# An attention stage that handles its two heads one after the other, with double-buffered score banks and weights, instead of side by side

## The chip, the cores and the metric

The kernel runs as one program on all 8 cores of one Trainium2 chip. Each core computes its own share and no core waits for another. The metric is the device time of the slowest core in microseconds (us), lower is better. The engines are TensorE (PE in the profile, PEld for its weight loads), ScalarE (ACT), VectorE (DVE), GpSimd (POOL) and SyncE (SP). SyncE only issues DMAs here, and GpSimd too.

## What is computed

The input x has the shape (4, 8192, 1024). Cut to what matters:

```python
xn = layernorm(x)
# attention, 16 heads of 64, 4096 keys and values, the same for every batch
q = relu(xn @ Wq.T + bq); k = relu(keys @ Wk.T + bk); v = relu(values @ Wv.T + bv)
a = softmax(q_h @ k_h.T / 8) @ v_h          # per head
a = transpose(a, (0, 1, 3, 2)).reshape(q.shape)
s = a + xn
# mixture of 8 experts, top 2, then a layernorm, then silu
g = silu(layernorm(xn + sum_e w_e * (relu(xn @ W1_e.T + b1_e) @ W2_e.T + b2_e)))
y = x + s * g
```

Core c takes batch c // 2 and, of it, 8 of the 16 heads with all 8192 queries. Because a head's result is transposed and reshaped, 8 heads are exactly 4096 rows of the output, so that each core finishes its own 4096 rows.

## The kernel before, in words

The program is written engine by engine: each stage has one block of instructions per engine (`@blk.tensor`, `@blk.scalar` and so on), and the order in a block is the order on that engine. Semaphores (`wait_ge`, `bump`) tie them together. There is no scheduler. The stages are, in order: keys and values projected (K transposed in `KT`, V in `VV`, both resident), phase A (layernorm, Q projected and stored to `d_qts`), the attention stage, and the expert stage. The change touches the attention stage alone.

**Work of the attention stage.** There are four head pairs `hp`. A pair has its 64 + 64 rows of Q in one tile `bQ` (128 partitions, 8192 queries). A pair runs 16 query tiles `qt` of 512 queries. A query tile runs 16 groups `gr`, each of two chunks of 128 keys. For one group TensorE multiplies four score products, alternately for head A on partitions 0 to 63 (L547, into `pScA`) and head B on partitions 64 to 127 (L550, into `pScB`). ScalarE turns `pScA` and then `pScB` (128 x 1024 each) into exponentials in `bEx` (L600, L603). TensorE then multiplies them with `bVE`, V with a column of ones, into `pAvA` and `pAvB` (L561; the last group L574), of which row 64 is the softmax's denominator. There is one `pScA` and one `pScB`, and the scores of a group wait for both exponentials of the group before. TensorE issues the values' products of a group after the scores of the next one.

**End of a query tile.** VectorE copies `pAvA` and `pAvB` out in four copies (L645 to L648), rows to `bAssy` and denominators to `bDnS`. The next tile's first score waits for all four. GpSimd bounces them to HBM in three DMAs in a row, each waiting for the one before (L482, L486, L490). `bAssy` has two halves, so the copies of a tile wait for the bounce of two tiles earlier.

**End of a pair (the head tail).** For each of its two heads SyncE loads `bXr` (2 MB of x), the denominators `bD8` (L517) and the bounced result `bScr` (2 MB, L523). TensorE repeats the denominators over the partitions (L586, L587, `pDb`), VectorE takes the reciprocal (L653), multiplies (L658) and adds (L663), ScalarE normalizes x (L611) and then issues the store of `bScr` to `d_ss` (L618). There is one of each buffer, so that the second head's loads wait for the first head's adds and store. After both, VectorE fills `bVE` for the next pair (L632), from which the next pair's first score waits.

**The casts.** GpSimd's block begins each pair with four DMAs, two of W1 and two of W2 (L473, L476), each reading 16 MB of fp32 weights and writing 8 MB of bf16 for the expert stage. They wait only for the one before of the same kind, and stand ahead of the pair's bounces.

Of the kernel before, what the change touches and what calls it, by code (L numbers as in the profile page):

```python
# [17 lines left out]
S = 8192  # L18
# [20 lines left out]
def build_program():  # L39
# [37 lines left out]
    with ExitStack() as st0:  # L77
        def sb(name, shape, dt):
            return st0.enter_context(nc.sbuf_tensor(name, shape, dt))
        def sem(name):  # L80
            return Ctr(st0, nc, name)
# [32 lines left out]
        c_qT = sem("c_qT"); c_xr = sem("c_xr"); c_d8 = sem("c_d8"); c_scr = sem("c_scr")  # L114
# [326 lines left out]
        def sc_cnt(hp, qt, gr):  # L441
            return (hp * NQT + qt) * NGR + gr + 1
        def ex_cnt(hp, qt, gr):
            return ((hp * NQT + qt) * NGR + gr + 1) * 2
        def av_cnt(hp, qt, gr):
            return (hp * NQT + qt) * NGR + gr + 1
        def ae_cnt(hp, qt):
            return (hp * NQT + qt + 1) * 4
        def bn_cnt(hp, qt):
            return 48 * (hp * NQT + qt + 1)  # L450

        with ExitStack() as stb:
            bQ = stb.enter_context(nc.sbuf_tensor("bQ", [128, S], BF16))
            bVE = stb.enter_context(nc.sbuf_tensor("bVE", [128, 2 * 32 * 65], BF16))
            bEx = stb.enter_context(nc.sbuf_tensor("bEx", [128, 4 * 1024], BF16))
            bAssy = stb.enter_context(nc.sbuf_tensor("bAssy", [128, 2 * 512], F32))
            bDnS = stb.enter_context(nc.sbuf_tensor("bDnS", [1, 4 * 512], F32))
# [4 lines left out]
            pScA = stb.enter_context(nc.psum_tensor("pScA", [128, 1024], F32))  # L462
            pScB = stb.enter_context(nc.psum_tensor("pScB", [128, 1024], F32))
            pAvA = stb.enter_context(nc.psum_tensor("pAvA", [128, 512], F32))
            pAvB = stb.enter_context(nc.psum_tensor("pAvB", [128, 512], F32))
# [3 lines left out]
            def _(g):  # L469
                for hp in range(4):  # L470
# [7 lines left out]
                    for qt in range(NQT):  # L478
                        g.wait_ge(b_ae.h, ae_cnt(hp, qt))
                        sl = qt % 2  # L480
                        g.wait_ge(c_bn.h, c_bn.n)
                        g.dma_start(out=d_bnc[:, qt * 512:(qt + 1) * 512],  # L482
                                    in_=bAssy[:, sl * 512:(sl + 1) * 512]).then_inc(c_bn.h, 16)
                        c_bn.n += 16
                        g.wait_ge(c_bn.h, c_bn.n)
                        g.dma_start(out=d_bncr2[0:1, qt * 512:(qt + 1) * 512],  # L486
                                    in_=bDnS[0:1, (sl * 2) * 512:(sl * 2 + 1) * 512]).then_inc(c_bn.h, 16)
                        c_bn.n += 16
                        g.wait_ge(c_bn.h, c_bn.n)
                        g.dma_start(out=d_bncr2[1:2, qt * 512:(qt + 1) * 512],  # L490
                                    in_=bDnS[0:1, (sl * 2 + 1) * 512:(sl * 2 + 2) * 512]).then_inc(c_bn.h, 16)
                        c_bn.n += 16
            W1CAST, W2CAST = c_w1.n, c_w2.n

            @blk.sync
            def _(sync):
                for hp in range(4):
# [5 lines left out]
                    if hp >= 1:  # L503
                        sync.wait_ge(b_sc.h, sc_cnt(hp - 1, NQT - 1, NGR - 1))
                    c_qT.bump(sync.dma_start(out=bQ[:], in_=d_qts[hp]), 16)
                    for a in range(2):
# [7 lines left out]
                        sync.wait_ge(c_bn.h, bn_cnt(hp, NQT - 1))  # L514
# [16 lines left out]
            def _(t):  # L531
                for hp in range(4):
                    t.wait_ge(c_qT.h, 16 * (hp + 1))
                    t.wait_ge(b_ve.h, 2 * (hp + 1))
                    for qt in range(NQT):
                        if qt >= 1:
                            t.wait_ge(b_ae.h, ae_cnt(hp, qt - 1))
                        elif hp >= 1:
                            t.wait_ge(b_ae.h, ae_cnt(hp - 1, NQT - 1))
# [579 lines left out]
```

## Time and profile before

| | us |
|---|---|
| median of 4 runs | 13927.75 (13821.23 to 14802.28) |
| the other two runs | 13857.45, 13998.06 |
| the profiled execution, its time | 13778.97 |
| the profiled execution, its span on the slowest core | 13777.0 |
| spans of the eight cores | 13734.0 to 13777.0 |

The profile is one execution, recorded on core 0. Its time and its span differ by 2 us. All rows shown are of that core. In a row of the timeline the columns are: start in us, duration in us, engine, line and operation, output and inputs, how many instructions are merged, and in brackets how long the engine stood idle before it and what ended that. "PEclk" is the granted TensorE clock as a share of 2.4 GHz, so 0.50 is the lower level of 1.2 GHz.

### The profile page before, as it was taken

The page shows a single profiled execution, that of the slowest core. Times are in us where ns is not written, and L with a number is a line of the kernel's source. Part 1 is how long each engine was busy: PE and PEld are TensorE (multiplying, and loading weights), DVE is VectorE, ACT ScalarE, POOL GpSimd, SP SyncE. Part 2 cuts the span into 40 slices and gives each one's busy share as a digit, 9 for nine tenths or more (in the row PEclk, how much of TensorE's full clock was granted, in tenths as well). Part 3 has the DMA queues.
Part 4 walks back from the last instruction along what each step waited for, and adds up shares of the span by engine and source line. Part 5 has one row for each costly group of instructions (what it writes and reads, how often), then busy time and mean ns, then how long its engine had stood idle before and what let it go on. Part 6 is the DMA issues. An engine that isn't in the chain of part 4 may idle for free.

```text
span 13777.0 us, 118078 instructions; the slowest of 8 cores (13734.0 to 13777.0 us)
## 1 busy us (share of the span) xinstructions
PE 9561.0 (69%) x43120; PEld 4159.8 (30%) x43808; DVE 2433.7 (18%) x5384; ACT 4015.3 (29%) x4988; POOL 159.4 (1%) x297
## 2 busy tenths in 40 slices
PE   3235552254055135499799799799799799798897
PEld 1124110011011011144344344344344344343343
DVE  0345000000000000211211211211211211212212
ACT  1232562365066146411211211211211211211212
POOL 0000000000000000000000000000000000000000
PEclk7675896688589678799899899899899899899998
DMA  8521005401800720144344344344344344343343
GB/s 115 102 72 65 19 5 65 81 6 18 127 6 6 85 61 6 53 147 147 141 150 147 129 149 152 130 150 150 135 147 150 140 148 150 128 150 141 141 150 116
DMA packets 244726, 1438.74 MB, mean 104 GB/s; under 512 B 25581, under 2 KB 66806, under 8 KB 108102
## 3 DMA queue, kind: packets, MB, share of 16 engines
q1 hardware_dynamic: 178646, 1176.04, 23.7%
q0 software_dynamic: 39920, 204.77, 10.6%
q10 hardware_dynamic: 25600, 50.34, 1.0%
q8 instruction: 367, 6.01, 0.2%
q14 instruction: 193, 1.58, 0.0%
HBM read 1517.84 MB, written 201.59 MB: 125 GB/s over the span
## 4 chain that ended last, share of the span: by engine, by line
PE 60%; ACT 17%; another core or an unknown queue 10%; DVE 8%; issue 4%; DMA 1%; ACTq 0%; DVEq 0%; SPq 0%; POOLq 0%
PE pO L819 26%; PE pH L799 25%; ACT bEx L600 8%; ACT bEx L603 7%; PE pScA L547 5%; DVE aXnT L325 1%; PE pQL L425 1%; PE pQL L417 1%; DVE aSm L295 1%; DVE aVar L303 1%; PE pScB L550 0%; DVE aXnT L329 0%; PE pTr L409 0%; DMA bD<-bncr 0%
## 5 line engine op out<-in xcount | busy, mean ns | idle before, releaser
L799 PE MATMUL pH<-cXnT,cW 128*128 128x512 bf16 x16053 | 3560.8, 381 | 241.0 <-ACT cHR L852 222.2
L819 PE MATMUL pO<-cHW,cW 128*128 128x512 bf16 x16053 | 3538.3, 379 | 108.8 <-DVE cHW L942 91.0
L852 ACT ACTIVATE cHR<-pH,cB 128x512 bf16<-128x512 f32 x2048 | 1405.8, 687 | 5441.6 <-PE pH L799 5365.3
L799 PEld LDWEIGHTS pH<-cXnT,cW 128*128 128x128 bf16 x16384 | 1604.9, 98 | 2181.8 <-issue 283.4
L819 PEld LDWEIGHTS pO<-cHW,cW 128*128 128x128 bf16 x16384 | 1593.8, 98 | 2036.7 <-issue 131.7
L547 PE MATMUL pScA<-bQ,KT 64*128 64x512 bf16 x2048 | 680.5, 415 | 1469.7 <-ACT bEx L603 1195.1
L600 ACT ACTIVATE bEx<-pScA 128x1024 bf16<-128x1024 f32 x1024 | 1048.6, 1024 | 1338.0 <-PE pScB L550 1338.0
L942 DVE TENSOR_TENSOR cHW<-cHR,cWbc 128x512 bf16<-128x512 bf16 x2048 | 871.0, 425 | 2689.3 <-ACT cHR L852 2689.3
L603 ACT ACTIVATE bEx<-pScB 128x1024 bf16<-128x1024 f32 x1024 | 1041.8, 1017 | 0.0
L956 DVE TENSOR_TENSOR cAcc<-pO,cAcc 128x512 f32<-128x512 f32 x448 | 309.8, 692 | 2852.6 <-PE pO L819 2784.2
L547 PEld LDWEIGHTS pScA<-bQ,KT 64*128 64x128 bf16 x2048 | 132.6, 94 | 1992.0 <-issue 1992.0
L586 PE MATMUL pDb<-bD,cRep 8*128 8x512 f32 x16 | 16.3, 1121 | 1028.1 <-DMA bD<-bncr 1028.1
L550 PE MATMUL pScB<-bQ,KT 64*128 64x512 bf16 x2048 | 696.9, 424 | 0.0
L409 PE MATMUL pTr<-cIdF,aXn 128*128 128x128 f32 x768 | 174.7, 387 | 724.7 <-ACT aXn L367 677.3
L561 PE MATMUL pAvA<-bEx,bVE 128*65 128x512 bf16 x1920 | 640.8, 418 | 0.0
L561 PE MATMUL pAvB<-bEx,bVE 128*65 128x512 bf16 x1920 | 607.2, 400 | 0.0
L645 DVE COPY bAssy<-pAvA 64x512 f32<-64x512 f32 x64 | 43.7, 683 | 3097.5 <-PE pAvB L574 3097.5
L409 PEld LDWEIGHTS pTr<-cIdF,aXn 128*128 128x128 f32 x768 | 126.5, 199 | 774.7 <-issue 771.2
L611 ACT ACTIVATE bXr<-bXr,stBL,stRS 128x1024 f32<-128x1024 f32 x32 | 37.0, 1231 | 1028.5 <-DMA bXr<-xo 656.2
L586 PEld LDWEIGHTS pDb<-bD,cRep 8*128 8x128 f32 x16 | 4.0, 306 | 1036.1 <-issue 1036.1
L561 PEld LDWEIGHTS pAvB<-bEx,bVE 128*65 128x65 bf16 x1920 | 226.7, 118 | 228.6 <-issue 49.5
L830 PE MATMUL pT<-cIdF,cAcc 128*128 128x128 f32 x256 | 51.2, 367 | 336.6 <-DVE cT L972 328.2
(107 smaller groups left out, 3114.9 us busy)
## 6 DMA issues: line engine op xcount, KB each, us to landing
cW<-w1b SPq DMA_DIRECT2D x512, 1024.0 KB, 6.4
cW<-w2b SPq DMA_DIRECT2D x512, 1024.0 KB, 6.3
w1b<-w1t POOLq DMA_DIRECT2D x8, 8192.0 KB, 128.3
w2b<-w2t POOLq DMA_DIRECT2D x8, 8192.0 KB, 161.6
aX<-x SPq DMA_DIRECT2D x16, 2048.0 KB, 7.9
aX<-xo SPq DMA_DIRECT2D x8, 2048.0 KB, 7.9
bXr<-xo SPq DMA_DIRECT2D x8, 2048.0 KB, 13.3
bnc<-bAssy POOLq DMA_DIRECT2D x64, 256.0 KB, 2.3
```

What stands on the lines that cost most here:

```text
L295: vf.bump(v.reduce_sum(aSm[:, i:i + 1], xb[:, i * 1024:(i + 1) * 1024], axis=AX.X), 1)
L409: inst = t.transpose(p[:, dcq * 128:(dcq + 1) * 128], aXn[:, i * 1024 + dc * 128: i * 1024 + (dc + 1) * 128], cIdF[:])
L547: t.matmul(pScA[:, col], KT[0:64, hp * TKV + tc * 128: hp * TKV + (tc + 1) * 128], bQ[0:64, qt * 512:(qt + 1) * 512], start=True, stop=True)
L550: inst = t.matmul(pScB[:, col], KT[64:128, hp * TKV + tc * 128: hp * TKV + (tc + 1) * 128], bQ[64:128, qt * 512:(qt + 1) * 512], start=Tru ...
L561: inst = t.matmul(pav[0:65, :], bVE[:, (a * 32 + tc) * 65:(a * 32 + tc + 1) * 65], bEx[:, (a * 2 + grm % 2) * 1024 + tcl * 512: (a * 2 + g ...
L600: inst = s.activation(bEx[:, (gr % 2) * 1024:(gr % 2 + 1) * 1024], pScA[:], AF.Exp, scale=0.125)
L603: inst = s.activation(bEx[:, (2 + gr % 2) * 1024:(2 + gr % 2 + 1) * 1024], pScB[:], AF.Exp, scale=0.125)
L799: inst = t.matmul(pH[fc % 3][:], cW1[ug % 3][:, ((fc % 4) * 8 + dc) * 128: ((fc % 4) * 8 + dc + 1) * 128], xnb[:, dc * 512:(dc + 1) * 512] ...
L819: inst = t.matmul(pO[dc % 2][:], cW2[vg % 3][:, fc * 128:(fc + 1) * 128], cHW[:, fc * 512:(fc + 1) * 512], start=(first and fc == 0), stop ...
L852: inst = s.activation(cHR[:, (fc % 3) * 512:(fc % 3 + 1) * 512], pH[fc % 3][:], AF.Relu, bias=cB1[:, e * 32 + fc:e * 32 + fc + 1])
L942: inst = v.tensor_tensor(cHW[:, fc * 512:(fc + 1) * 512], cHR[:, (fc % 3) * 512:(fc % 3 + 1) * 512], cWbc[:, (e % 2) * 512:(e % 2 + 1) * 5 ...
L956: inst = v.tensor_tensor(cAcc[:, dc * 512:(dc + 1) * 512], pO[dc % 2][:], cAcc[:, dc * 512:(dc + 1) * 512], ALU.add)
```

## The change

The attention stage now runs one head at a time. The unit of work is `u`, two chunks of 128 keys of one head: two score products (L548), one exponential of 128 x 1024, two value products (L566, L577). There are 4 pairs x 2 heads x 16 query tiles x 16 units = 2048 units. `pSc` has two buffers, used in turn, and `bEx` has four; the score products of a unit wait for the exponential of two units earlier. `bQ` and `bVE` are doubled: SyncE loads the next pair's queries at the start of a pair, VectorE fills `bVE` for two pairs at the start and for pair hp + 2 at the end of pair hp. A query tile's result is one copy of 65 rows (L646), bounced in two DMAs. The head tail is deferred on two engines: TensorE's products for `pDb` stand in the third unit of the next head, ScalarE's store stands at the third query tile of the next head. VectorE's part of the tail stands between the last copy of its head and the first copy of the next. The casts keep their place ahead of each pair's bounces.

The core of the diff (the loops of scores and values, the eviction, the bounce):

```diff
-            bQ = stb.enter_context(nc.sbuf_tensor("bQ", [128, S], BF16))
-            bVE = stb.enter_context(nc.sbuf_tensor("bVE", [128, 2 * 32 * 65], BF16))
+            bQ = [stb.enter_context(nc.sbuf_tensor(f"bQ{i}", [128, S], BF16)) for i in range(2)]
+            bVE = [stb.enter_context(nc.sbuf_tensor(f"bVE{i}", [128, 2 * 32 * 65], BF16)) for i in range(2)]
...
-            pScA = stb.enter_context(nc.psum_tensor("pScA", [128, 1024], F32))
-            pScB = stb.enter_context(nc.psum_tensor("pScB", [128, 1024], F32))
+            pSc = [stb.enter_context(nc.psum_tensor(f"pSc{i}", [128, 1024], F32)) for i in range(2)]
...
+                    for a in range(2):
+                        for qt in range(NQT):
+                            g.wait_ge(b_ae.h, ev_idx(hp, a, qt))
+                            sl = qt % 2
+                            g.wait_ge(c_bn.h, c_bn.n)
+                            g.dma_start(out=d_bnc[64 * a:64 * a + 64, qt * 512:(qt + 1) * 512],
+                                        in_=bAssy[0:64, sl * 512:(sl + 1) * 512]).then_inc(c_bn.h, 16)
...
+                            g.dma_start(out=d_bncr2[a:a + 1, qt * 512:(qt + 1) * 512],
+                                        in_=bAssy[64:65, sl * 512:(sl + 1) * 512]).then_inc(c_bn.h, 16)
...
+                    for a in range(2):
+                        for qt in range(NQT):
+                            for u in range(NU):
+                                gu = gu_of(hp, a, qt, u)
+                                if gu >= 2:
+                                    t.wait_ge(b_ex.h, gu - 1)
+                                for tcl in range(2):
+                                    tc = u * 2 + tcl
+                                    inst = t.matmul(
+                                        pSc[u % 2][:, tcl * 512:(tcl + 1) * 512],
...
+                                b_sc.bump(inst, 1)
...
+                                if qt == 0 and u == 2 and pending_tail:
+                                    emit_tail(pending_tail.pop())
+                                if u >= 1:
+                                    um = u - 1
+                                    t.wait_ge(b_ex.h, gu)
+                                    if um == 0 and (hp * 2 + a >= 1 or qt >= 1):
+                                        t.wait_ge(b_ae.h, ev_idx(hp, a, qt) - 1)
...
+                            if qt == 2 and pending_store:
+                                emit_store(pending_store.pop())
+                            for u in range(NU):
+                                gu = gu_of(hp, a, qt, u)
+                                s.wait_ge(b_sc.h, gu + 1)
+                                if gu >= 4:
+                                    s.wait_ge(b_av.h, gu - 3)
+                                inst = s.activation(bEx[:, (gu % 4) * 1024:(gu % 4 + 1) * 1024],
+                                                    pSc[u % 2][:], AF.Exp, scale=0.125)
...
+                        for qt in range(NQT):
+                            v.wait_ge(b_av.h, gu_of(hp, a, qt, NU - 1) + 1)
+                            sl = qt % 2
+                            if ev_idx(hp, a, qt) >= 3:
+                                v.wait_ge(c_bn.h, 32 * (ev_idx(hp, a, qt) - 2))
+                            b_ae.bump(v.tensor_copy(bAssy[0:65, sl * 512:(sl + 1) * 512],
+                                                    pAv[a][0:65, :]), 1)
```

What stands in a row on TensorE in the middle of a query tile before: four scores, then the four value products of the group before. The names are the product's output and its two inputs.

```order
L547 MATMUL pScA<-bQ,KT 128x512 [waits b_ex]
L550 MATMUL pScB<-bQ,KT 128x512
L547 MATMUL pScA<-bQ,KT 128x512
L550 MATMUL pScB<-bQ,KT 128x512
L561 MATMUL pAvA<-bEx,bVE 65x512 [waits b_ex]
L561 MATMUL pAvA<-bEx,bVE 65x512
L561 MATMUL pAvB<-bEx,bVE 65x512 x2
```

And what stands there now, in the same place:

```order
L548 MATMUL pSc0<-bQ0,KT 128x512 [waits b_ex]
L548 MATMUL pSc0<-bQ0,KT 128x512
L566 MATMUL pAv0<-bEx,bVE0 65x512 [waits b_ex]
L566 MATMUL pAv0<-bEx,bVE0 65x512
L548 MATMUL pSc1<-bQ0,KT 128x512 [waits b_ex]
L548 MATMUL pSc1<-bQ0,KT 128x512
L566 MATMUL pAv0<-bEx,bVE0 65x512 [waits b_ex]
L566 MATMUL pAv0<-bEx,bVE0 65x512
```

The two heads' scores no longer alternate, and scores and values change places every two products instead of every four. On TensorE at the passage from the first head (`pAv0`) to the second (`pAv1`) of the first pair there stands now:

```order
L577 MATMUL pAv0<-bEx,bVE0 65x512 [waits b_ex]
L577 MATMUL pAv0<-bEx,bVE0 65x512
L548 MATMUL pSc0<-bQ0,KT 128x512 [waits b_ex]
L548 MATMUL pSc0<-bQ0,KT 128x512
L548 MATMUL pSc1<-bQ0,KT 128x512 [waits b_ex]
L548 MATMUL pSc1<-bQ0,KT 128x512
L566 MATMUL pAv1<-bEx,bVE0 65x512 [waits b_ex,b_ae]
L566 MATMUL pAv1<-bEx,bVE0 65x512
L548 MATMUL pSc0<-bQ0,KT 128x512 [waits b_ex]
L548 MATMUL pSc0<-bQ0,KT 128x512
L533 MATMUL pDb<-bD8,cRep8 128x512 [waits c_d8]
L534 MATMUL pDb<-bD8,cRep8 128x512
```

The products for `pDb` moved from behind the last query tile of a pair into the next head's third unit, with their wait for the denominators' load. On GpSimd at the start of the second pair the casts and the first bounce now stand like this:

```order
L466 DMA w1b<-w1t 256x16384 [waits c_w1]
L469 DMA w2b<-w2t 256x16384 [waits c_w2]
L466 DMA w1b<-w1t 256x16384 [waits c_w1]
L469 DMA w2b<-w2t 256x16384 [waits c_w2]
L476 DMA bnc<-bAssy 64x512 [waits b_ae,c_bn]
L480 DMA bncr<-bAssy 16x1x32 [waits c_bn]
```

The casts kept their place; behind them stand two DMAs per query tile of one head, where three per query tile of a pair stood.

## Rows read from the trace of the kernel before

**Rows 1.** Windows by stage: stretch, its length, busy PE, PEld, DVE, ACT, POOL, PEclk, DMA.

```profile
1401.00:5815.00 4414.00, 1818.86 (x8224) 549.16 (x8224) 324.31 (x600) 2027.89 (x2104) 106.92 (x205) 0.80 0.25 40
5815.00:13777.00 7962.00, 7193.07 (x32522) 3254.32 (x33184) 1635.81 (x3166) 1656.63 (x2347) 33.22 (x64) 0.96 0.39 143
2600.00:3300.00 700.00, 379.38 (x1745) 114.85 (x1745) 38.32 (x56) 423.70 (x438) 20.92 (x41) 0.90 0.02 6
```

**Rows 2.** The page's groups: the first exponential, its mean duration and idle time before.

```profile
L600 ACT ACTIVATE bEx<-pScA 128x1024 bf16<-128x1024 f32 x1024 | 1048.6, 1024 | 1338.0 <-PE pScB L550 1338.0
```

**Rows 3.** Timeline, one group in the middle of a query tile.

```profile
3107.51 0.37 PE L547 MATMUL pScA<-bQ,KT 64*128 64x512 bf16 x1 [1.25 <-ACT bEx L603]
...
3107.72 0.37 PE L547 MATMUL pScA<-bQ,KT 64*128 64x512 bf16 x1
3107.74 0.38 PE L550 MATMUL pScB<-bQ,KT 64*128 64x512 bf16 x1
3108.05 0.62 PE L561 MATMUL pAvA<-bEx,bVE 128*65 128x512 bf16 x2
3108.27 1.02 ACT L600 ACTIVATE bEx<-pScA 128x1024 bf16<-128x1024 f32 x1 [0.90 <-PE pScB L550]
...
3108.50 0.59 PE L561 MATMUL pAvB<-bEx,bVE 128*65 128x512 bf16 x2
3109.19 1.02 ACT L603 ACTIVATE bEx<-pScB 128x1024 bf16<-128x1024 f32 x1
3110.35 0.37 PE L547 MATMUL pScA<-bQ,KT 64*128 64x512 bf16 x1 [1.25 <-ACT bEx L603]
```

**Rows 4.** Timeline, the passage from the first query tile to the second.

```profile
1452.71 0.69 DVE L648 COPY bDnS<-pAvB 1x512 f32<-1x512 f32 x1
...
1453.65 0.58 PE L547 MATMUL pScA<-bQ,KT 64*128 64x512 bf16 x1 [3.19 <-DVE bDnS L648]
...
1457.30 0.63 PE L547 MATMUL pScA<-bQ,KT 64*128 64x512 bf16 x1
...
1457.89 1.06 PE L561 MATMUL pAvA<-bEx,bVE 128*65 128x512 bf16 x2
...
1458.74 1.06 PE L561 MATMUL pAvB<-bEx,bVE 128*65 128x512 bf16 x2
```

**Rows 5.** Timeline, from the first pair's last exponential to the second pair's first score.

```profile
2216.07 1.02 ACT L603 ACTIVATE bEx<-pScB 128x1024 bf16<-128x1024 f32 x1
...
2228.19 0.57 POOL L476 DMA_DIRECT2D w2b<-w2t  x1
2312.30 0.55 POOL L473 DMA_DIRECT2D w1b<-w1t  x1 [83.54 <-DMA w1b<-w1t]
2393.02 0.55 POOL L476 DMA_DIRECT2D w2b<-w2t  x1 [80.17 <-DMA w2b<-w2t]
...
2402.27 4.63 DVE L658 TENSOR_TENSOR bScr<-bScr,bDiv 128x1024 f32<-128x1024 f32 x4 [145.93 <-DMA bScr<-bnc]
...
2580.12 0.58 PE L547 MATMUL pScA<-bQ,KT 64*128 64x512 bf16 x1 [22.67 <-DVE bVE L635]
```

**Rows 6.** Timeline, tail after the last pair; then the expert stage's first weight load.

```profile
5739.75 4.62 ACT L611 ACTIVATE bXr<-bXr,stBL,stRS 128x1024 f32<-128x1024 f32 x4
...
5744.66 0.58 POOL L482 DMA_DIRECT2D bnc<-bAssy  x1 [45.66 <-DVE bDnS L648]
5747.58 0.49 POOL L486 DMA_DIRECT2D bncr<-bDnS  x1 [2.35 <-DMA bnc<-bAssy]
5749.65 0.48 POOL L490 DMA_DIRECT2D bncr<-bDnS  x1 [1.57 <-DMA bncr<-bDnS]
...
5753.72 2.04 PE L586 MATMUL pDb<-bD,cRep 8*128 8x512 f32 x2 [12.69 <-DMA bD<-bncr]
...
5757.57 6.56 DVE L653 RECIPROCAL bDiv<-pDb 128x1024 f32<-128x1024 f32 x1 [13.54 <-PE pDb L587]
...
L732 SPq DMA_DIRECT2D cW<-w1b x512: 319/320/1702, 5814.8 to 13609.7; - x171
```

More of the change, by code:

```diff
@@ L531, in _, with emit_tail @@
             def _(t):
+                pending_tail = []
+                def emit_tail(h):
+                    t.wait_ge(c_d8.h, 16 * (h + 1))
+                    if h >= 1:
+                        t.wait_ge(b_rc.h, h)
+                    t.matmul(pDb[:, 0:512], cRep8[:], bD8[:, 0:512], start=True, stop=True)
+                    inst = t.matmul(pDb[:, 512:1024], cRep8[:], bD8[:, 512:1024],
+                                    start=True, stop=True)
+                    b_dn.bump(inst, 1)
@@ L574, in _ @@
                                 inst = t.matmul(
[L575 to L578 removed]
+                                    pAv[a][0:65, :],
+                                    bVE[hp % 2][:, (a * 32 + tc) * 65:(a * 32 + tc + 1) * 65],
@@ L579, in _ @@
+                                    bEx[:, (gu % 4) * 1024 + tcl * 512:
+                                           (gu % 4) * 1024 + (tcl + 1) * 512],
                                     start=False, stop=(tcl == 1))
-                        b_av.bump(inst, 1)
-                    for a in range(2):
-                        h = 2 * hp + a
-                        t.wait_ge(c_d8.h, 16 * (h + 1))
-                        if h >= 1:
-                            t.wait_ge(b_rc.h, h)
-                        t.matmul(pDb[:, 0:512], cRep8[:], bD8[:, 0:512], start=True, stop=True)
-                        inst = t.matmul(pDb[:, 512:1024], cRep8[:], bD8[:, 512:1024],
-                                        start=True, stop=True)
-                        b_dn.bump(inst, 1)
+                            b_av.bump(inst, 1)
@@ L615, in _ @@
                             b_xn.bump(inst, 1)
[L616 to L620 removed]
+                        pending_store.append(h)
+                emit_store(pending_store.pop())
@@ L650, in _ @@
+                ve_fill(0)
+                ve_fill(1)
+                for hp in range(4):
                     for a in range(2):
                         h = 2 * hp + a
+                        for qt in range(NQT):
+                            v.wait_ge(b_av.h, gu_of(hp, a, qt, NU - 1) + 1)
[4 more added lines that the diff above has]
+                                                    pAv[a][0:65, :]), 1)
```

179 lines of the change are left out of this document (62 added, 117 removed).

## The prediction

> **What bounds the kernel now.** I read the windows by stage first. The attention stage takes 4414 us, from 1401 to 5815, and the expert stage the 7962 us behind it [rows 1]. The change leaves the second alone, so only the 4414 us can move. In them no engine is full: ScalarE is busy for 2028 us and TensorE for 1819 us. So the stage is bound by waits between engines, and the next views are the page's groups and the timeline.
>
> The groups say that ScalarE stands idle for 1338 us ahead of the first exponential, always for the scores [rows 2]. The timeline shows the cycle. Scores start at 3107.51, the exponentials at 3108.27 and 3109.19, and the next scores at 3110.35, which waited 1.25 us for the second exponential [rows 3]. A group is two head-units and takes 2.84 us, of which ScalarE stands for 0.90: 1.42 us a unit, strictly scores, then exponentials, then scores. At a query tile's end TensorE stands for another 3.19 us behind four copies of about 0.7 us, and the products after that idle time run with starts some 0.43 us apart instead of 0.21, the lower of the two clock levels [rows 4].
>
> The last part is the pair boundary. The last exponential of pair one ends at 2217.1, the first score of pair two starts at 2580.1: 363 us without attention work. GpSimd had issued two casts by 2228.2; the first landed 84 us later, the second another 81 us on, when the fourth was issued (2393.0). VectorE waited 146 us for `bScr` until 2402.3, under that traffic [rows 5]. There are three such boundaries.
>
> **Term 1: the unit in the steady state.** The change removes the wait of a group's scores for both exponentials. A unit's scores wait for the exponential of two units earlier, so two chains run interleaved. I walk one of them, from the end E of an exponential, with the durations of rows 3. TensorE starts 0.14 us behind it (3109.19 + 1.02 = 3110.21, against 3110.35). Ahead of the unit's own scores it now has the two value products: 0.24 (the first pair of values starts at 3108.05 and the second at 3108.50, 0.45 for two, so 0.24 + 0.21), then a passage to the scores. The opposite passage, scores to values, took 3108.05 - 3107.74 = 0.31. No row shows values to scores without a wait between. From below it costs an ordinary step of 0.21, from above it drains the product before, 0.38. I take the nearest row, 0.31. Then 0.21 to the second score, 0.37 to its end, 0.15 to ScalarE (3107.74 + 0.38 = 3108.12 against 3108.27), and 1.02 for the exponential. The sum is 0.14 + 0.24 + 0.31 + 0.21 + 0.37 + 0.15 + 1.02 = 2.44 us for two units, 1.22 a unit.
>
> Two other limits stand below that. ScalarE alone needs 0.92 a unit (3108.27 to 3109.19). TensorE alone needs 0.24 + 0.31 + 0.21 + 0.31 = 1.07. The alternation of heads, two score products at once in two halves of the array, is lost: before, four score products started within 0.23 us [rows 3], now two need 0.21 between their starts, twice for two units. That is in the 1.07, which stays under 1.22, so the chain hides it.
>
> The Trainium skill, TensorEngine Tiling (Array Packing), section Tiling Modes, speaks against this change: changing the tiling mode drains TensorE, and scores of 64 rows and values of 128 are two modes that now alternate every two products. The trace shows 0.31 where a full drain would be 0.38, so agrees in part. By the rule at its full price a cycle would be 2.51 us instead of 2.44, some 70 us over the stage.
>
> **Term 2: the query tile.** At its end the last values wait for the last exponential, and only then come the next tile's scores, so both chains are at one point. The first exponential starts 2.44 us after the last one. The second follows at 1.07 (TensorE's limit), and 14 more come at 7 x 2.44. A tile is 1.07 + 17.08 + 2.44 = 20.6 us. The one copy of 0.7 us ends before the first exponential does, 1.4 + 1.02 us later, so it is hidden; if VectorE is late, as below, it isn't. TensorE never stands still for more than about 1.3 us in a tile, and behind idle times of 1.25 us the products still ran at the upper level [rows 3], so I take the upper level throughout. 128 tiles x 20.6 = 2637 us. Before, 64 tiles took (2217 - 1401) / 16 = 51 us each, 3264 us.
>
> **Term 3: the passage inside a pair, 4 times.** I count from T, the start of the row at 5739.75, where the last exponential is ending [rows 6]. The bounce was issued 4.9 us later, behind four copies and four products; with one copy and two products it is 3 x 0.72 + 0.43 less, T + 2.3. The denominators' bounce comes 2.9 later. One bounce of 2.07 (5747.58 to 5749.65) is gone, so `pDb` starts 6.14 - 2.07 = 4.1 later, T + 9.3, and takes 3.85: T + 13.1. Behind this wait on TensorE stand the next head's second value products and its fourth scores, and ScalarE waits for those; without the wait the fourth exponential would be at T + 4.9, with it at about T + 14.4. ScalarE's 4.6 us for `bXr` [rows 6] lie within it. So 9.5 us, and some 3 us for products at the lower clock behind it: 12.5 x 4 = 50 us. VectorE's part ends at T + 13.1 + 6.7 + 9.6 = T + 29.4 (reciprocal, four multiplies and four adds at 4.63 and 0.17 for a start [rows 5, 6]), and the first copy of the next head is due at about T + 31. That is just covered. ScalarE's store waits for VectorE's adds too, but stands at the third tile, some 20 us later, and SyncE's loads for the next head are needed only at its end.
>
> **Term 4: the pair boundary, 3 times.** The casts are issued behind the last bounce, about T + 5.6. They need 4 x 81 us, T + 330. Two more DMAs share the time: `bScr` and the early `bQ`, 2 MB each; I add 5 us for `bQ`. VectorE waits for `bScr` as it does now, until 2402.3 - 2217.1 = 185 less 5 us for the earlier issue, T + 180, then 9.6 us, and 5.8 us to fill `bVE`. Behind that wait stands the copy of the next pair's first tile, and TensorE's second tile waits for it. So the first tile is copied at about T + 196, the second is done by T + 215, the third by T + 236. The third tile's copy needs the first tile's bounce. GpSimd can issue it once the second W2 cast has begun (T + 171), but its bytes lie behind two casts in the same queue, since rows 5 show casts of that queue landing one after the other at 81 us each. It lands at about T + 340. Then three tiles and two units stand done, 3 x 20.6 + 2.4 = 64 us. Loss 276, with 6 for two restarts at the lower clock 282 us; three times 846 us. Before it was 363 us.
>
> The Trainium skill, DMA: Bandwidth & Descriptors, section Queues, rings and completion order, says that an engine consumes one ring in order and takes turns between rings. The trace agrees: the casts land in turn, while `bScr` on SyncE's queue lands among them.
>
> **Term 5: the end.** One head's tail: T + 29.4, then store and wait. Before, the last adds end at 5757.57 + 6.7 + 9.6, and a second head's tail follows, up to 5814.8 [rows 6]. I take 8 us from adds to the first expert load, so 37 us. The start is unchanged, 3 us until the first exponential.
>
> **The sum.** 3 + 2637 + 50 + 846 + 37 = 3573 us, so the stage ends at 4974 instead of 5814.8, 840 us earlier. 13779 - 840 = 12939 us for an execution like the profiled one. That one lay 149 us below the median of the runs shown (13928), and 42, 78 and 219 below the three nearest ones. I add 80 us: 13,020 us.
>
> **The rivals.**
>
> The bounce isn't held up by the casts. For it speaks that it is small and its engine is free from T + 171. Against it speak the casts that land in turn. The boundary would end with VectorE at T + 196, loss 175 instead of 282, and the time would be 13,020 - 320 = 12,700.
>
> The two chains don't overlap, and the unit stays at today's 1.42 us. Something that I count as parallel isn't, such as a weight load of a half-array product beside a full-array one. A tile is 22.7 us, + 2.1 x 128 = 270: 13,290. For it speaks only that no row shows this alternation.
>
> TensorE's clock stays at its lower level in the stage: this is the side on which the kernel becomes slower, and the place is every unit. At that level products start 0.43 apart, and from the last score to the first value it is 0.59 (1457.30 to 1457.89) [rows 4]. TensorE alone then needs 0.43 + 0.41 + 0.43 + 0.59 = 1.86 us a unit, more than any chain, or 29.7 us a tile: 9.1 x 128 = 1165 more, so 14,185, slower by just under 2% of the median of before. It decides from 1.22 + 840 / 2048 = 1.63 us a unit on. For it speaks that the stage has a mean of 0.80 granted [rows 1]. Against it speaks that this is from idle times of 3 us and the boundaries, that a full stretch of tiles has 0.90, and that TensorE's idle time shrinks; the expert stage, where it is 90% busy, has 0.96.
>
> That the change doesn't do what it says (deferring the tail leaves it in the path) is in terms 3 and 4 already: inside a pair it costs 12 us and at a boundary it hides only three tiles.
>
> **How the numbers follow.** The forecast has 0.76, the rival of the free bounce 0.09, the unit at 1.42 has 0.09, and the lower clock 0.06, half of it on either side of the 2% line. The forecast's own bounds are 1.17 to 1.26 us a unit (0.21 or 0.38 for the passage), -115 to +75 us, 40 us either way for the three boundaries, and 80 us for which run it is compared with: 12,840 to 13,180. To hold 8 in 10 with room for the two near rivals I reach from 12,760 to 13,260. A measurement of this kernel can tell about 2% from no change, 13,650 and 14,210 around 13,928. Faster by over 2% hold the forecast and the two near rivals: 0.94. Within 2%: 0.03. Slower by over 2%: 0.03. These are the clock rival's two halves.
>
> **What would show it.** Exponentials start in pairs 2.44 us apart, with ScalarE's idle time before each about 0.2 us instead of 0.90 per two. First exponentials of tiles 20.6 us apart. In the second tile of a new pair TensorE waits for the copy for about 150 us, and in the fourth for about 100 us. The granted clock in a stretch of tiles is above 0.90. The expert stage takes 7962 us. I am wrong if the unit is above 1.3 us, or if the boundary costs less than 240 us.

## The result, and the profile after

The changed kernel is slower: 3.2% by the comparison of runs on the same chips (ratio 1.0321, 95% interval 1.0264 to 1.0377). Its runs took 14247 to 14338 us, those of the kernel before 13821 to 13998. In some executions of any kernel the cores of a die ran at a lower granted clock and took some per cent longer, and neither the times nor the rows given here are from such cores in the stage that is read. I had forecast 13,020 us and a range of 12,760 to 13,260; the result lies outside, on the other side of no change. The rows of the changed kernel are those of core 4, with a span of 14243.1 us.

The windows by stage, in the columns of [rows 1]:

```profile
1401.00:6281.00 4880.00, 4033.78 (x8224) 676.63 (x8224) 238.95 (x499) 2124.10 (x2100) 141.53 (x268) 0.50 0.23 36
6281.00:14243.00 7962.00, 7227.90 (x33184) 3253.09 (x33184) 1636.38 (x3168) 1657.34 (x2351) 33.53 (x64) 0.96 0.39 143
4100.00:4400.00 300.00, 291.56 (x598) 48.49 (x598) 6.18 (x9) 151.58 (x149) 9.48 (x18) 0.50 0.02 4
```

The expert stage takes 7962 us, to the microsecond what it took in [rows 1]. The attention stage grew from 4414 to 4880 us, and 466 us is the whole loss. In it the same work (8224 products recorded in both) keeps TensorE busy for 4034 us instead of 1819. The granted clock is 0.50, the lower level of 1.2 GHz, in the stage as a whole (on each of the eight cores, without a break) and so in a stretch in the middle of a head, where TensorE is busy for 291.56 of 300 us. Before, such a stretch had 0.90 with TensorE busy for 379 of 700 us.

The timeline in that stretch, core 4, next to [rows 3]:

```profile
4100.20 1.06 PE L566 MATMUL pAv<-bEx,bVE 128*65 128x512 bf16 x2
4100.43 1.02 ACT L606 ACTIVATE bEx<-pSc 128x1024 bf16<-128x1024 f32 x1 [0.93 <-PE pSc L548]
...
4101.20 1.03 PE L548 MATMUL pSc<-bQ,KT 64*128 64x512 bf16 x2
...
4102.16 1.06 PE L566 MATMUL pAv<-bEx,bVE 128*65 128x512 bf16 x2
4102.38 1.02 ACT L606 ACTIVATE bEx<-pSc 128x1024 bf16<-128x1024 f32 x1 [0.93 <-PE pSc L548]
...
4103.15 1.03 PE L548 MATMUL pSc<-bQ,KT 64*128 64x512 bf16 x2
```

A unit takes 1.95 us (4100.43 to 4102.38) where I had 1.22. TensorE's rows have no idle time in brackets at all, and ScalarE stands for 0.93 us before each exponential. So the wait that the change was to remove is gone, and TensorE at its lower clock has taken its place as the bound. The two value products, and the two score products, take 0.96 to 1.00 us to the start of the pair of products behind them.

The pair boundary, GpSimd's queue and then VectorE's, core 4. The last exponential of pair one ends at 2445.2:

```profile
2451.83 0.56 POOL L469 DMA_DIRECT2D w2b<-w2t  x1
2535.75 0.55 POOL L466 DMA_DIRECT2D w1b<-w1t  x1 [83.36 <-DMA w1b<-w1t]
2615.63 0.55 POOL L469 DMA_DIRECT2D w2b<-w2t  x1 [79.33 <-DMA w2b<-w2t]
2641.11 0.56 POOL L476 DMA_DIRECT2D bnc<-bAssy  x1 [24.93 <-DVE bAssy L646]
2777.07 0.51 POOL L480 DMA_DIRECT2D bncr<-bAssy  x1 [135.40 <-DMA bnc<-bAssy]
```

```profile
2639.81 0.69 DVE L646 COPY bAssy<-pAv 65x512 f32<-65x512 f32 x1
2670.60 0.69 DVE L646 COPY bAssy<-pAv 65x512 f32<-65x512 f32 x1 [30.11 <-PE pAv L577]
2778.74 0.69 DVE L646 COPY bAssy<-pAv 65x512 f32<-65x512 f32 x1 [107.45 <-DMA bncr<-bAssy]
```

These answer to [rows 5]. The bounce of the first tile, 128 KB, was issued at 2641.1 and took 136 us behind two casts in its queue. The third tile's copy waited 107 us for it. That is the mechanism of term 4, at the place and nearly at the time forecast.

The tail after the last head, core 4, next to [rows 6]:

```profile
6244.65 4.62 ACT L613 ACTIVATE bXr<-bXr,stBL,stRS 128x1024 f32<-128x1024 f32 x4
...
6253.93 2.04 PE L533 MATMUL pDb<-bD,cRep 8*128 8x512 f32 x2 [7.99 <-DMA bD<-bncr]
...
6281.46 1.77 SPq L729 DMA_DIRECT2D cW<-w1b  x3
```

From 6244.65 it is 9.3 us to `pDb` and 36.8 us to the expert stage's first load. Both are the forecast's figures.

So one question is left: why does TensorE run at 1.2 GHz for a stage of 4.9 ms, in whose tiles it is 97% busy?

### The profile page after: what moved, and what is told of

Read it like the earlier page. It is cut to its first block, busy times and chain, and to the rows that moved or that the text cites. A ratio compares the mean times of both kernels' runs of the same rounds, so it can differ in the third digit from the quotient of the medians.

```text
span 15369.4 us, 123111 instructions; the slowest of 8 cores (14221.4 to 15369.4 us)
## 1 busy us (share of the span) xinstructions
PE 12944.6 (84%) x43808; PEld 4547.1 (30%) x43808; DVE 2345.7 (15%) x5256; ACT 4114.4 (27%) x4988; POOL 194.3 (1%) x361
## 3 DMA queue, kind: packets, MB, share of 16 engines
q1 hardware_dynamic: 178646, 1176.04, 20.8%
## 4 chain that ended last, share of the span: by engine, by line
PE 79%; another core or an unknown queue 8%; DVE 6%; ACT 4%; issue 2%; DMA 1%; ACTq 0%; DVEq 0%; POOL 0%; POOLq 0%; SPq 0%
PE pO L816 27%; PE pH L796 27%; PE pSc L548 11%; PE pAv L566 11%; ACT bEx L606 2%; DVE aXnT L326 1%; PE pAv L577 1%; PE pQL L418 1%; PE pQL L426 1%; DVE aSm L296 1%; DVE aVar L304 1%; DMA bD<-bncr 0%; PE pTr L410 0%; DVE aXnT L330 0%
## 5 line engine op out<-in xcount | busy, mean ns | idle before, releaser
L796 PE MATMUL pH<-cXnT,cW 128*128 128x512 bf16 x16384 | 4141.1, 423 | 219.2 <-ACT cHR L849 219.2
L816 PE MATMUL pO<-cHW,cW 128*128 128x512 bf16 x16384 | 4120.8, 421 | 90.7 <-DVE cHW L939 90.7
L606 ACT ACTIVATE bEx<-pSc 128x1024 bf16<-128x1024 f32 x2048 | 2083.2, 1024 | 2724.0 <-PE pSc L548 2724.0
L566 PE MATMUL pAv<-bEx,bVE 128*65 128x512 bf16 x3840 | 2037.2, 633 | 712.7 <-DVE bAssy L646 627.0
L796 PEld LDWEIGHTS pH<-cXnT,cW 128*128 128x128 bf16 x16384 | 1734.9, 106 | 2608.2 <-issue 2118.8
L816 PEld LDWEIGHTS pO<-cHW,cW 128*128 128x128 bf16 x16384 | 1724.1, 106 | 2467.4 <-issue 1954.2
L548 PE MATMUL pSc<-bQ,KT 64*128 64x512 bf16 x4096 | 2089.4, 619 | 10.5 <-DMA bQ<-qts 10.5
L566 PEld LDWEIGHTS pAv<-bEx,bVE 128*65 128x65 bf16 x3840 | 361.2, 145 | 2329.1 <-issue 2329.1
L548 PEld LDWEIGHTS pSc<-bQ,KT 64*128 64x128 bf16 x4096 | 281.7, 109 | 1626.5 <-issue 1626.5
L646 DVE COPY bAssy<-pAv 65x512 f32<-65x512 f32 x128 | 87.9, 687 | 4070.3 <-PE pAv L577 3754.6
L869 ACT ACTIVATE cTh<-cT,nNm 128x1024 f32<-128x1024 f32 x32 | 36.8, 1149 | 632.9 <-DVE nNm L976 632.9
L326 DVE CAST aXnT<-pTr 128x128 bf16<-128x128 f32 x768 | 180.9, 280 | 66.9 <-PE pTr L410 65.6
L577 PE MATMUL pAv<-bEx,bVE 128*65 128x512 bf16 x256 | 132.5, 621 | 42.0 <-ACT bEx L606 42.0
```

The lines of the kernel that those rows point to most:

```text
L326: a_ev.bump(v.tensor_copy(aXnT[:, dc * 512 + i * 128: dc * 512 + (i + 1) * 128], p[:, dcq * 128:(dcq + 1) * 128]), 1)
L548: inst = t.matmul(pSc[u % 2][:, tcl * 512:(tcl + 1) * 512], KT[64 * a:64 * a + 64, hp * TKV + tc * 128: hp * TKV + (tc + 1) * 128], bQ[hp ...
L566: inst = t.matmul(pAv[a][0:65, :], bVE[hp % 2][:, (a * 32 + tc) * 65:(a * 32 + tc + 1) * 65], bEx[:, ((gu - 1) % 4) * 1024 + tcl * 512: (( ...
L577: inst = t.matmul(pAv[a][0:65, :], bVE[hp % 2][:, (a * 32 + tc) * 65:(a * 32 + tc + 1) * 65], bEx[:, (gu % 4) * 1024 + tcl * 512: (gu % 4) ...
L606: inst = s.activation(bEx[:, (gu % 4) * 1024:(gu % 4 + 1) * 1024], pSc[u % 2][:], AF.Exp, scale=0.125)
L796: inst = t.matmul(pH[fc % 3][:], cW1[ug % 3][:, ((fc % 4) * 8 + dc) * 128: ((fc % 4) * 8 + dc + 1) * 128], xnb[:, dc * 512:(dc + 1) * 512] ...
```

## The experiments

The score products of one head fill 64 of the array's 128 rows. Before, head A's on rows 0 to 63 and head B's on rows 64 to 127 ran side by side; the change made them follow each other on one half. That is theory H (for the halves). The other suspects were the change between 64-row and 128-row products, which now comes every two products (theory M, for the mode), and the high busy share itself (theory B). All but e6 and e7 compute other sums than the reference and serve as measurements only. All experiments but e4, e6 and e7 are edits of the changed kernel.

**e1, score products over all rows.** The scores then sum both heads; the number of products is the same.

```diff
-                                        KT[64 * a:64 * a + 64,
+                                        KT[0:128,
-                                        bQ[hp % 2][64 * a:64 * a + 64, qt * 512:(qt + 1) * 512],
+                                        bQ[hp % 2][0:128, qt * 512:(qt + 1) * 512],
```

> The changed kernel with its score products over all 128 rows instead of one head's 64 (the result then mixes both heads). Counts, columns and order stay; no product uses half an array and the tiling mode never changes. Theory H (the clock stays low because the score products fill only one half of the rows at a time): granted clock of the attention tiles near 1.00, unit about 1.2 us, stage about 3600 us. Theory M (the clock stays low because the tiling mode changes every two products): the same, since the changes go too. Theory B (it is held low because TensorE is nearly always busy): 0.50, unit 1.7 to 1.75 us.

**e2, the two score products of a unit on different halves.**

```diff
-                                        KT[64 * a:64 * a + 64,
+                                        KT[64 * tcl:64 * tcl + 64,
-                                        bQ[hp % 2][64 * a:64 * a + 64, qt * 512:(qt + 1) * 512],
+                                        bQ[hp % 2][64 * tcl:64 * tcl + 64, qt * 512:(qt + 1) * 512],
```

> The changed kernel with the first score product of a unit on rows 0 to 63 and the second on rows 64 to 127 (the result mixes both heads). The order, the counts and the mode changes stay; the two products can run side by side, as before the change. H: granted clock near 1.00, unit about 1.2 us, stage about 3600 us. M: 0.50, unit 1.6 to 1.9 us. B: 1.00 only if side-by-side products lower the busy share enough; at 0.50 the unit would be about 1.55 us.

**e3, value products over 64 rows too.**

```diff
-                                            bVE[hp % 2][:, (a * 32 + tc) * 65:(a * 32 + tc + 1) * 65],
+                                            bVE[hp % 2][64 * a:64 * a + 64, (a * 32 + tc) * 65:(a * 32 + tc + 1) * 65],
```

(and `bEx` on the same rows)

> The changed kernel with its value products over 64 rows, the same 64 as the head's scores (half of the keys are left out of the values' sum). No mode changes any more, and all products are on one half of the rows. H: 0.50, unit about 1.72 us (four starts 0.43 apart). M: near 1.00, unit about 1.15 us. B: 0.50.

**e4, the kernel before, with head B's scores on head A's half.**

```diff
-                                                KT[64:128, hp * TKV + tc * 128: hp * TKV + (tc + 1) * 128],
-                                                bQ[64:128, qt * 512:(qt + 1) * 512], start=True, stop=True)
+                                                KT[0:64, hp * TKV + tc * 128: hp * TKV + (tc + 1) * 128],
+                                                bQ[0:64, qt * 512:(qt + 1) * 512], start=True, stop=True)
```

> The kernel before with head B's score products on rows 0 to 63 too, so that no two run side by side (head B's result is then head A's scores). Nothing else differs. H: the granted clock of the tiles falls from 0.90 to 0.50, a group takes about 4.1 us instead of 2.84, total 14,900 to 15,200 us. M and B: the clock stays at 0.90, a group takes about 3.25 us (0.4 for two starts), total about 14,200 us.

Measured: the same window, 1500 to 2000 us, in e1 (core 6), e2, e3 and e4 (core 0), in this order. The last columns are the granted clock and the DMA share:

```profile
1500.00:2000.00 500.00, 391.55 (x1585) 134.54 (x1583) 32.74 (x34) 389.75 (x400) 26.30 (x50) 0.99 0.06 20
```

```profile
1500.00:2000.00 500.00, 379.53 (x1651) 96.78 (x1650) 33.66 (x35) 405.64 (x416) 26.88 (x51) 0.99 0.07 20
```

```profile
1500.00:2000.00 500.00, 477.93 (x1103) 160.30 (x1102) 27.48 (x26) 283.96 (x279) 17.90 (x34) 0.50 0.05 18
```

```profile
1500.00:2000.00 500.00, 419.54 (x906) 109.64 (x904) 19.14 (x28) 219.01 (x226) 10.92 (x21) 0.51 0.01 4
```

e1 and e2 have 0.99, e3 and e4 have 0.50 and 0.51. e2 keeps every change between 64 and 128 rows and has the high clock; e3 has none and the low one: theory M falls. e2 is high with TensorE 76% busy, e4 is low with 84%, e3 with 96%; e4 was the exact converse, the rows of head B's two operands moved in the old kernel, and took 14971 to 15106 us over the cores where 13734 to 13777 stood. Theory B doesn't fit the expert stage, which is 91% busy at 0.96 while e4 is less busy at half the clock. Theory H predicted the clock of all four, and the time of e4; for the stage of e1 and e2 it had about 3600 us, and up to the first expert load they took about 3410 and 3320. The 0.51 of e4 has a reason. On each of its cores the clock rose 16 to 19 times for a few us, 1% of the stage, in 134 of 138 cases at the end of a query tile. There eight value products over all 128 rows stand without a score product between them (on core 0 from 1591.84 to 1595.89). The spans of e2 are 12648 to 12680 us: with the halves side by side, the structure of the change is 8% faster than before.

The two periods of e2, core 0, to be laid beside the timeline of the changed kernel:

```profile
1850.56 1.94 ACT L606 ACTIVATE bEx<-pSc 128x1024 bf16<-128x1024 f32 x2 [0.30 <-PE pSc L548]
1850.93 0.39 PE L548 MATMUL pSc<-bQ,KT 64*128 64x512 bf16 x2
1851.73 0.59 PE L566 MATMUL pAv<-bEx,bVE 128*65 128x512 bf16 x2 [0.41 <-ACT bEx L606]
1852.25 0.39 PE L548 MATMUL pSc<-bQ,KT 64*128 64x512 bf16 x2
1852.64 0.59 PE L566 MATMUL pAv<-bEx,bVE 128*65 128x512 bf16 x2
1852.80 1.94 ACT L606 ACTIVATE bEx<-pSc 128x1024 bf16<-128x1024 f32 x2 [0.30 <-PE pSc L548]
1853.17 0.39 PE L548 MATMUL pSc<-bQ,KT 64*128 64x512 bf16 x2
```

Two score products together last 0.39 us, and two units 2.24 us (1850.56 to 1852.80), 1.12 a unit.

**e5, alternate halves unit by unit** (`64 * (u % 2)` in place of `64 * a` in both operands). Inside a tile the halves are then never used side by side.

> The changed kernel with both score products of an even unit on rows 0 to 63 and both of an odd unit on rows 64 to 127 (the result mixes both heads). Both halves are used, but never side by side. Theory H1 (what counts is that the two halves work at the same time, so the array is full in each microsecond): granted clock of the tiles 0.50, unit about 1.95 us, as in the changed kernel. Theory H2 (it is enough that both halves are used in turn): near 1.00, unit about 1.2 us.

**e8, value products over 128 columns.**

```diff
-                                            pAv[a][0:65, :],
-                                            bVE[hp % 2][:, (a * 32 + tc) * 65:(a * 32 + tc + 1) * 65],
+                                            pAv[a][0:128, :],
+                                            bVE[hp % 2][:, min((a * 32 + tc) * 65, 4032):min((a * 32 + tc) * 65, 4032) + 128],
```

> The changed kernel with value products that fill all 128 columns instead of 65 (the 63 more are not used by anyone). The score products stay on one half of the rows. Theory H1: 0.50, unit about 1.95 us. Theory A (the clock follows the filled share of the whole array, rows times columns, over time): the value products now fill 1.0 instead of 0.51, more than the side-by-side scores gave back in e2, so near 1.00, unit about 1.2 us.

Windows of e5 (core 3), then e8 (core 0):

```profile
1500.00:1900.00 400.00, 379.02 (x798) 61.28 (x796) 8.24 (x12) 202.45 (x199) 12.64 (x24) 0.50 0.02 4
```

```profile
1500.00:1900.00 400.00, 388.91 (x807) 54.74 (x806) 8.24 (x12) 204.36 (x202) 13.14 (x25) 0.50 0.02 5
```

Both took about what the changed kernel takes (14301 and 14371 us). e8 has 0.50 on all eight cores for the whole stage, as the changed kernel and e3 have. e5 doesn't: core 3 shows 0.50 in this window, but core 2 shows 0.56.

```profile
1500.00:1900.00 400.00, 373.14 (x827) 62.23 (x826) 8.93 (x13) 214.04 (x211) 13.69 (x26) 0.56 0.02 5
```

On every core of e5 the clock rose 41 to 62 times, for 3 to 5% of the stage, and all but two of these rises began within 1 us behind the copy of a tile. The passage from tile to tile is the one place where e5 is not what its name says. There the scores of two units stand in a row, two products on each half, and run side by side after all: four together last 1.04 us, where the changed kernel's four last 1.89. Core 2:

```profile
1709.38 1.04 PE L548 MATMUL pSc<-bQ,KT 64*128 64x512 bf16 x4
1711.84 0.59 PE L566 MATMUL pAv<-bEx,bVE 128*65 128x512 bf16 x2 [1.42 <-ACT bEx L606]
...
1714.29 1.04 PE L566 MATMUL pAv<-bEx,bVE 128*65 128x512 bf16 x2 [0.17 <-ACT bEx L606]
```

The value products take 0.59 us behind the passage, as at the upper level, and 1.04 again two units later. So e5 speaks for H1 twice: with the halves used in turn the clock is low, and it rises where they come side by side. Theory H2, near 1.00, falls. Filling more columns in the value products doesn't make up for half the rows in the scores, so theory A falls too.

**e9, the first 8 tiles of each head as in e2, the last 8 as in the changed kernel** (`ro = 64 * tcl if qt < 8 else 64 * a`).

> The changed kernel with the first 8 query tiles of every head as in e2 (the two score products of a unit on different halves) and the last 8 as in the changed kernel, on one half; no wait stands between them. It tells whether one-half products pull a high clock down, or only fail to raise a low one. H1 strictly (they pull it down): 1.00 in tiles 1 to 8, 0.50 in tiles 9 to 16, of about 19 and 32 us each, total about 13,500 us. Rival L (a latch: once up, the denser work at the upper level keeps it up): 1.00 in all 16 tiles, about 20 us each for the second 8, total about 12,750 us.

Windows of core 4, in the first head's tiles 1 to 8 and 9 to 15, then in the second head up to its tenth tile:

```profile
1410.00:1560.00 150.00, 115.27 (x498) 29.00 (x496) 5.49 (x8) 121.85 (x125) 8.47 (x16) 0.99 0.03 8
1565.00:1750.00 185.00, 179.59 (x368) 29.83 (x368) 4.12 (x6) 93.47 (x92) 6.31 (x12) 0.50 0.02 5
...
1860.00:2010.00 150.00, 118.36 (x496) 29.48 (x496) 4.81 (x7) 122.01 (x125) 7.88 (x15) 1.00 0.04 10
```

The copies at tile ends, same core, tiles 8 and 9 of the first head, and 9 to 11 of the second:

```profile
1552.51 0.69 DVE L647 COPY bAssy<-pAv 65x512 f32<-65x512 f32 x1 [18.53 <-PE pAv L578]
1583.51 0.69 DVE L647 COPY bAssy<-pAv 65x512 f32<-65x512 f32 x1 [30.32 <-PE pAv L578]
...
1991.58 0.69 DVE L647 COPY bAssy<-pAv 65x512 f32<-65x512 f32 x1 [20.08 <-PE pAv L578]
2012.34 0.69 DVE L647 COPY bAssy<-pAv 65x512 f32<-65x512 f32 x1 [20.08 <-PE pAv L578]
2033.40 0.69 DVE L647 COPY bAssy<-pAv 65x512 f32<-65x512 f32 x1 [20.37 <-PE pAv L578]
```

Neither expectation is met as written. In the first head the clock fell within one tile (31.0 us from copy to copy). In the second, one-half tiles went on at the upper level, at 20.8 us each. Over the 8 cores and 8 heads, going by the times between copies (tiles 9 to 16), the upper level lasted through all of them in 4 of 64 cases; in 26 the tenth tile was already a slow one, in the other 34 a later one was the first. Once fallen it rose in no case before the next side-by-side tile. By the record of the granted clock, all 60 falls began 1.7 to 3.1 us behind the copy of a tile, and none inside a tile. That is the passage where both chains are at one point and TensorE stands still, for 0.99 us in the rows below. The one behind the eighth tile of the first head, core 4:

```profile
1552.26 1.03 PE L549 MATMUL pSc<-bQ,KT 64*128 64x512 bf16 x4
1554.29 0.59 PE L567 MATMUL pAv<-bEx,bVE 128*65 128x512 bf16 x2 [0.99 <-ACT bEx L607]
1554.82 0.60 PE L549 MATMUL pSc<-bQ,KT 64*128 64x512 bf16 x2
...
1556.14 1.03 PE L549 MATMUL pSc<-bQ,KT 64*128 64x512 bf16 x2
```

So one-half products that ran at the upper level held the clock inside a tile, lost it at one of the next passages in 60 of 64 cases, and never raised it again. The side-by-side tiles of the same kernel have the same kind of passage and hold 0.99 over eight of them. The total, 13206 us, lies between the two expectations.

Two more kernels ask what the change's idea is worth if the halves stay side by side.

**e6, the kernel before with a unit of one chunk for both heads.** The core of the edit (the exponentials, the two copies of 65 rows and their bounces follow it):

```diff
+                    for g in range(NQT * NCH):
+                        qt, tc = g // NCH, g % NCH
+                        gu = hp * NQT * NCH + g
+                        if gu >= 2:
+                            t.wait_ge(b_ex.h, gu - 1)
+                        for a in range(2):
+                            inst = t.matmul(
+                                pSc[gu % 2][:, a * 512:(a + 1) * 512],
+                                KT[64 * a:64 * a + 64, hp * TKV + tc * 128: hp * TKV + (tc + 1) * 128],
+                                bQ[64 * a:64 * a + 64, qt * 512:(qt + 1) * 512], start=True, stop=True)
+                        b_sc.bump(inst, 1)
+                        if g >= 2:
+                            values(g - 2)
```

> A version of the kernel before whose unit is one chunk of 128 keys for both heads: two side-by-side score products into one of two buffers, one exponential over both heads, values two units later; tile result copied in two copies of 65 rows. Head tails, casts and loads as before. H1: the tiles keep a clock near 1.00, ScalarE is the bound with 0.92 to 0.97 us a unit, a tile about 32 us instead of 51, boundaries 363 us as before: stage about 3250 us, total about 12,600 us, ratio to before about 0.91. If the clock fell to 0.50 a unit would be about 1.5 us and the total about 13,700 us.

Measured: ratio 0.9063 (0.9024 to 0.9102), at 12471 and 12472 us. Window and timeline, core 0:

```profile
1500.00:1900.00 400.00, 374.92 (x1641) 107.83 (x1640) 16.70 (x26) 382.26 (x414) 27.91 (x53) 0.99 0.04 10
```

```profile
1849.49 7.56 ACT L569 ACTIVATE bEx<-pSc 128x1024 bf16<-128x1024 f32 x8
1849.86 0.39 PE L542 MATMUL pSc<-bQ,KT 64*128 64x512 bf16 x2
...
1850.77 0.39 PE L542 MATMUL pSc<-bQ,KT 64*128 64x512 bf16 x2
```

Eight exponentials run as one row without a gap: ScalarE is the bound, and inside a tile a unit takes 0.91 to 0.92 us (1849.86 to 1850.77 on TensorE). A tile takes 30.5 us for both heads, where before it took 51 and the changed kernel takes 64.4 for two. That e6's loop is faster than e2's (0.92 against 1.12) I put down to its scores being issued ahead of the older values; no run has this difference alone.

**e7, e6 with the casts released one pair earlier and the bounces on SyncE's queue.**

```diff
+                    if hp >= 1:
+                        g.wait_ge(b_ae.h, 2 * (tile_of(hp - 1, 0) + 1))
                     for e in (2 * hp, 2 * hp + 1):
...
+                                for a2 in range(2):
+                                    co = (2 * sl + a2) * 512
+                                    c_bn.bump(sync.dma_start(out=d_bnc[64 * a2:64 * a2 + 64, qt * 512:(qt + 1) * 512],
+                                                             in_=bAssy[0:64, co:co + 512]), 16)
+                                    c_bn.bump(sync.dma_start(out=d_bncr2[a2:a2 + 1, qt * 512:(qt + 1) * 512],
+                                                             in_=bAssy[64:65, co:co + 512]), 16)
```

> e6 with the casts of pairs 1 to 3 released one pair earlier, behind the first tile's copy, and the bounces issued by SyncE on its own queue, four at once. If the boundary is 363 us because the casts run there, it falls to about 80 us (two head tails of some 35 us and the refill) and the total is about 12,600 - 850 = 11,750 us. Rival: a bounce takes longer than a tile beside the casts, and the tiles under them (some 330 us per pair) slow down by up to half: about 12,100 us.

Measured: ratio 0.8696 (0.8658 to 0.8733), the fastest version, at 11965 and 11968 us. That lies between the 11,750 us of the expectation and the 12,100 of its rival. SyncE's queue on core 2, in the first pair under the casts, then VectorE's wait for it:

```profile
1453.75 0.45 SPq L498 DMA_DIRECT2D bnc<-bAssy  x1
...
1521.39 0.45 SPq L498 DMA_DIRECT2D bnc<-bAssy  x1
```

```profile
1521.42 1.28 DVE L612 COPY bAssy<-pAv 65x512 f32<-65x512 f32 x2 [37.68 <-DMA bncr<-bAssy]
```

The next tile's bounces could only be issued 68 us after the last, when those had landed. So the rival came true in kind: four tiles of each of the first three pairs took 37 to 68 us, against 30.5 for a tile clear of the casts, which adds up to 114 to 121 us a pair. The boundary itself fell as expected, from 359 us in e6 (389.8 between the copies around it less a tile of 30.5) to 71. Three boundaries save about 860 us and the slow tiles give some 350 back. The stage, to the first expert load, ends at 3976 us on core 2 instead of 4471, a gain of 495 us of the 850 hoped for. A bounce on a queue of its own no longer waits behind two casts, but beside them it is still slow. Whether the shared engines or the memory make it so, no run tells.

## Why the prediction was wrong, step by step

**The step that failed** is one sentence of term 2: "so I take the upper level throughout". I had reasoned from idle times (none above 1.3 us, and 1.25 us had not lowered the clock in [rows 3]) and from busy shares. What decides here is whether the score products fill all rows at a time, by two halves side by side or by one product over all 128. e1, e2, e4 and e5 show that, and nothing but the rows of the scores' two operands moved in them. I had even noted in term 1 that the side-by-side running was lost, and priced it only as time in the array (hidden under the chain). Its real price was the clock: the next level down, for the whole stage.

The Trainium skill, TensorE: Matmul & The Clock Gate, Part 1, says that the clock is released when TensorE is busy. The trace of the changed kernel disagrees as it stands: 97% busy in a stretch of tiles, and 0.50 there and in the whole stage.

**The rival with the lower clock**, to which I gave 0.06, was the truth in its mechanism. That its total came so near, 14,185 against 14,247 us, is in part luck. Its tile of 29.7 us was 2.5 us short of the measured 32.2, which makes 320 us over the stage. The three boundaries made up for some 160 of it (688 us instead of 846), the passages inside a pair for 20, and the 80 us that I had added for the choice of run for 80 more. The tile was short in two places. The unit had 0.41 us for the passage from values to scores and 0.59 for the one back, in a sum of 1.86. Measured are 0.99 us from two values to the next score and 0.96 from two scores to the next value, where 2 x 0.43 is 0.86: either passage costs some 0.1 us more than an ordinary step at this clock, and the unit is 1.95. And 16 units alone were counted, without the end of a tile, where TensorE stands for about 1 us. In e3, without passages between 64 and 128 rows, the unit is 1.71 us, so that two of them cost 0.24. The Trainium skill, TensorEngine Tiling (Array Packing), section Tiling Modes, says that a change of the tiling mode drains TensorE. By the rows a full drain would cost 0.2 (a product lasts 0.63 us and the next starts 0.43 behind it), so the trace shows about half of it.

**Term 1 and 2, the unit and the tile**, were right for the clock that they assumed. The one-half tiles that e9 ran at the upper level took 20.8 us, forecast 20.6, and their scores start 2.45 us apart for two units, forecast 2.44 (core 4):

```profile
1993.89 0.60 PE L549 MATMUL pSc<-bQ,KT 64*128 64x512 bf16 x2
...
1996.34 0.60 PE L549 MATMUL pSc<-bQ,KT 64*128 64x512 bf16 x2
```

The walk along the chain from the durations of rows was sound, and the level that it started from was not.

**Term 3, the passage inside a pair.** `pDb` started 9.3 us behind T, as forecast. The time between the copies around it is 39.4 us, 7.2 above a tile; forecast 12.5 at the upper clock. In e2, at that clock, it is 28.7 to 30.1 against 18.9, so 10 to 11 us. Slightly too high.

**Term 4, the boundary.** In the changed kernel the third tile's copy came 334 us behind the last exponential, forecast about 340. The loss is 193.2 + 30.8 + 108.1 + 30.8 us (from the last copy of the old pair to the fourth of the new) less four tiles of 32.2: 234 us. In e2, at the clock I had assumed, it is 190.8 + 20.3 + 118.3 + 19.6 - 4 x 18.9 = 273, forecast 282. The rival of the free bounce (175) is refuted by the 135.4 us row.

**Term 5, the end**, was 36.8 us, forecast 37. The start took 10 us instead of 3, since the first score waited 11 us for the load of `bQ`.

**The range.** The bounds of 12,840 and 13,180 don't follow from the amounts named beside them: added up, these reach from 12,785 to 13,215. The wider range that was stated covers both, so nothing hangs on it.

**The sum with the right clock**: 128 x 32.2 + 4 x 7.2 + 3 boundaries (234, 232 and 222) + 37 + 10 at the start is 4885 us, measured 4880. The other terms of the working stand within the amounts above; one level of the clock moved the stage by 1.3 ms, from 3573 to 4880 us.

## What to carry to other kernels

When a change stops two half-array products from running side by side, ask first what it does to TensorE's clock, and only then what it costs in time. A stretch in which TensorE is busy nearly all the time and its starts are 0.43 us apart for 512 columns is not a full engine but a slow one. Double-buffer in such a way that the two row halves stay together: here by one chunk of keys for two heads (e6) instead of two chunks for one head, for the same score buffers, and ratios of 0.91 against 1.03.

## What the runs showed of the hardware

Products with 64 contraction rows on one row half had the granted clock at 0.50 for a whole stage of 4.9 ms on all eight cores, though TensorE was 97% busy in its tiles. It was so whether the products between them filled 65 or 128 columns (e8) or 64 rows (e3). With the halves used in turn (e5) it was at 0.50 for 95 to 97% of the stage, and rose for a few us at tile passages, where four scores ran side by side. Side by side (e2), or widened to all rows (e1), they had it at 0.99 in the tiles. Entered at the upper level, the one-half stream is not stable: in e9 it was gone in 60 of 64 cases before 8 tiles were over, each time at the passage between two tiles, after times that differed from core to core. What exactly the chip counts stays open; the runs tell only which streams rose and which fell.

A DMA of 128 KB took 136 us behind two casts in its own queue, and a tile's four bounces together 68 us on another queue beside them. The median of all 128 such bounces in the changed kernel is 2.2 us.
